# Attention on one core: the numerator's matmuls grouped over two steps, and two small matmul blocks moved a step earlier

## The reference

```python
q = (x @ wq_w + wq_b).reshape(bs, sl, KV_H, FACTOR, HEAD_DIM)
k = (x @ wk_w + wk_b).reshape(bs, sl, KV_H, HEAD_DIM)
v = (x @ wv_w + wv_b).reshape(bs, sl, KV_H, HEAD_DIM)
attn = jnp.einsum('bqhfd,bkhd->bhfqk', q, k) * scale
att = jax.nn.softmax(attn, axis=-1)
a = jnp.einsum('bhfqk,bkhd->bqhfd', att, v)
```

## Time and profile of the kernel before

| | |
|---|---|
| median of three runs | 2871.31 us |
| profiled execution, time | 2874.47 us |
| profiled execution, span from first to last instruction | 2872.7 us |
| busy: PE, DVE, ACT, POOL | 96%, 77%, 53%, 67% of the span |
| attention stage | about 635 to 2345 us |
| granted TensorE clock, 700 to 2300 us | 0.99 to 1.00 of full speed |

### The profile page before, as it was taken

The page is one execution under the profiler, slowest core; times in us unless marked ns, Lnnn a source line. Parts: engine busy times, 40 slices in busy tenths (PEclk is TensorE's granted clock), DMA queues, the critical chain, the costliest instruction groups (busy, mean ns, idle before and its releaser), DMA issues. The chain is left out here.

```text
span 2872.7 us, 48710 instructions
## 1 busy us (share of the span) xinstructions
PE 2771.2 (96%) x14638; PEld 1701.4 (59%) x14638; DVE 2197.9 (77%) x2775; ACT 1520.3 (53%) x2906; POOL 1925.5 (67%) x714
## 2 busy tenths in 40 slices
PE   7999999999999999999999999999999959999997
PEld 4788888874444444444444444444444427888886
DVE  4433333348999999999999999999999967666675
ACT  3211111117766666666666667667666733455443
POOL 2433333218999999999999999999999965111110
PEclk9999999999999999999999999999999979999998
DMA  7544444524433444443344334443434333333331
GB/s 263 180 140 140 139 139 139 155 85 122 95 88 85 94 94 89 86 98 83 88 96 94 89 85 94 92 90 87 98 83 92 65 106 114 111 100 98 110 110 66
DMA packets 167583, 307.60 MB, mean 107 GB/s; under 512 B 50000, under 2 KB 91408, under 8 KB 159376
## 3 DMA queue, kind: packets, MB, share of 16 engines
q1 hardware_dynamic: 158368, 240.05, 28.8%
q0 software_dynamic: 9072, 66.06, 11.3%
HBM read 159.12 MB, written 79.82 MB: 83 GB/s over the span
## 5 line engine op out<-in xcount | busy, mean ns | idle before, releaser
L1006 ACT ACTIVATE p_t<-st_ps 128x512 f32<-128x512 f32 x2048 | 1113.8, 596 | 464.1 <-PE st_ps L1126 392.1
L1026 DVE TENSOR_REDUCE mx<-s_ps 128x1 f32<-128x1024 f32 x1002 | 1172.7, 1209 | 111.8 <-PE s_ps L1100 103.4
L955 POOL TENSOR_TENSOR p_sum<-p_sum,p_t 128x2048 f32<-128x2048 f32 x256 | 1178.8, 4605 | 44.7 <-ACT p_t L1006 28.2
L1126 PE MATMUL st_ps<-q_st,k_st 98*128 98x512 f32 x2048 | 815.8, 438 | 24.5 <-ACT p_t L1006 18.9
L1126 PEld LDWEIGHTS st_ps<-q_st,k_st 98*128 98x128 f32 x2048 | 345.9, 188 | 618.7 <-ACT p_t L1006 515.8
L1100 PE MATMUL s_ps<-k_st,q_st 96*128 96x512 f32 x2004 | 633.3, 397 | 1.8 <-DVE mx L1026 1.5
L1140 PE MATMUL num_ps<-p_t,v_sb 128*32 128x512 f32 x4096 | 547.2, 606 | 0.9 <-ACT p_t L1006 0.9
L1100 PEld LDWEIGHTS s_ps<-k_st,q_st 96*128 96x128 f32 x2004 | 379.2, 189 | 74.2 <-DVE mx L1026 5.1
L495 POOL TENSOR_TENSOR o_lo<-side,o_hi 128x512 fp32r<-128x512 f32 x80 | 104.3, 1304 | 323.6 <-ACT o_hi L465 323.4
L955 POOL TENSOR_TENSOR p_sum<-p_t 128x2048 f32<-128x2048 f32 x64 | 312.6, 4885 | 12.0 <-ACT p_t L1006 12.0
L1041 DVE TENSOR_REDUCE two_sum<-p_t 128x512 f32<-128x1024 f32 x256 | 317.6, 1241 | 3.3 <-DMA p_sum<-two_sum 2.0
(11 more groups left out here) (138 smaller groups left out, 2889.9 us busy)
## 6 DMA issues: line engine op xcount, KB each, us to landing
p_sum<-two_sum POOLq DMA_DIRECT2D x63, 1024.0 KB, 7.0
q_st<-q_hi_d SPq DMA_DIRECT2D x128, 256.0 KB, 4.4
stage<-w_mod SPq DMA_DIRECT2D x48, 512.0 KB, 6.3
q_hi_d<-o_hi SPq DMA_DIRECT2D x64, 256.0 KB, 2.0
q_lo_d<-o_lo SPq DMA_DIRECT2D x64, 256.0 KB, 2.0
q_st<-q_lo_d SPq DMA_DIRECT2D x64, 256.0 KB, 4.1
att_d<-a_sb SPq DMA_DIRECT2D x128, 128.0 KB, 2.3
a_f<-att_d SPq DMA_DIRECT2D x32, 512.0 KB, 4.8
```

What stands on the lines that cost most here:

```text
L955: nc.gpsimd.tensor_tensor(total, before, p_t[:, kt, :, :], ALU.add).then_inc(sum_done, 1)
L1006: nc.scalar.activation(p_t[:, s, c, :], st_ps[:, c % 2, :], ACT.Exp, scale=SCALE)\
L1026: nc.vector.tensor_reduce(mx[:, slot % 2, e:e + 1], s_ps[:, e % 2, :], AX_X, ALU.max)\
L1126: nc.tensor.matmul(st_ps[:, c % 2, :], k_st[:, slot // 2, s * P:(s + 1) * P], q_st[:, slot, jj, h * QW:(h + 1) * QW], start=True, stop=True)\
```

## The change

PE no longer makes one numerator block at the start of each step. At the start of every even step it makes those of the two steps before, one behind the other; odd steps begin with scores 2 and 3 straight away. The turn of the maxima moves from step 5 to step 4 (ACT's part with it, DVE's part to step 5), and the denominator's block from step 7 to step 6. After the last pair both remaining numerator blocks are made. No instruction is added or dropped.

```diff
-    SUM_STEP = 7
+    SUM_STEP = 6
     DIVIDE_STEPS = (1, 2, 3)
     DIVIDE_AFTER = 2
-    TURN_STEP = 5
+    TURN_STEP = 4
@@
                     for s in range(STEPS):
-                        before = (pair, slot, s - 1) if s else (pair - 1, (slot - 1) % QR, STEPS - 1)
-                        if not (below(pair, 1) and s == 0):
-                            add_num(*before)
+                        if s % 2 == 0 and not (below(pair, 1) and s == 0):
+                            before = (pair, slot, s) if s else (pair - 1, (slot - 1) % QR, STEPS)
+                            for back in (2, 1):
+                                add_num(*before[:2], before[2] - back)
                         if s == SUM_STEP and not below(pair, 1):
                             add_sum(pair - 1, (slot - 1) % 2)
                         if s == TURN_STEP and not is_int(pair, NPAIR - 1):
@@
                 pairs(pe, do)
-                add_num(NPAIR - 1, QR - 1, STEPS - 1)
+                for back in (2, 1):
+                    add_num(NPAIR - 1, QR - 1, STEPS - back)
                 add_sum(NPAIR - 1, (NPAIR - 1) % 2)
                 add_two(NPAIR - 1)
```

## The result

The changed kernel takes 2969.36 us (median of four runs, 2965.07 to 2970.97) against 2870.93 us before: a ratio of 1.0337, 95% interval 1.0324 to 1.0350. It is 98 us slower. The forecast was 2974 us.

A forecast was written before the change was run, and what follows sets the result against it. PE's pace and ACT's hand-over through the two banks of `st_ps`, equally late, were taken as the bound. Hand-over's 94 us plus 63 x 0.15 made 103 us, added to 2871: 2974 us, range 2915 to 3030.

The forecast's parts named there:

- Double block to c2: Start of an even step: from first numerator matmul to scores 2, two blocks take 1.85 us, the second costing 0.85.
- The hand-over chain: Odd steps: scores 2 and 3 (c2', c3') wait for ACT's exponentials of c0' and c1', loading at 4.23 and 4.71 us.
- Next block: Two steps between numerator blocks on PE: 6.57 us against 6.20, 0.37 more, 94 us over 255 groups.
- DVE at 0.05 for a whole pair: Fourth entry of an odd step: DVE's backlog reaches it once, by 0.0 to 0.3 us; taken as 0.05 a pair.
- rival 3: Odd steps: DVE becomes the bound, each fourth entry waiting 0.3 us for a maximum; 3042 us, chance 0.08.
- PE's saving: PE's stream: joining two numerator blocks saves 0.37 us in two steps, 6.20 to 5.83.
- The turn: Turn of the maxima moved to step 4: waiting for step 3's last maximum costs 0 to 0.3 us, taken as 0.1.
- The denominator: Denominator's block moved from step 7 to 6: 0.85 us in either place, behind a block both times; no cost.
- Loop edges: Edges of the loop: their cost to PE and ACT stays the same, since no instruction is added.
- Signs: Trace after: blocks 6.5 to 6.6 us apart, odd-step loads idle, PE's share under 0.95, POOL waiting for ACT, pairs 27.6.

The follow-up runs named there:

- after_low: Changed kernel with both matmuls of an entry writing the same half of `s_ps` and the maximum taken of that half alone: 2943.6 us, ratio 1.0246.
- grouped_only: Changed kernel with the turn of the maxima set back to step 5 and the denominator's block to step 7: 2926.5 us, ratio 1.0188.
- odd_order: Changed kernel with one entry matmul of each odd step placed between scores 2 and scores 3: 2952.1 us, ratio 1.0277.
- the twins with four banks: Kernel before and changed kernel, each with four banks for the scores and maxima over half of each row: 2844.9 and 2843.6 us.
- those without POOL's limit: Single-block and grouped kernels with four banks, half maxima, POOL's additions of steps 6 and 7 left out, reciprocal of a constant: 2823.2 and 2721.4 us.
- the first relief of POOL: Single-block and grouped kernels with four banks, half maxima, no POOL additions of steps 6 and 7, multiplication by zero replacing the reciprocal: 2854.9 and 2796.4 us.
- the clean one: Rerun of the first relief of POOL with the reciprocal of a constant replacing the multiplication by zero: 2823.2 us single, 2721.4 us grouped.

## Why the prediction was right

The direction, the size and the mechanism held; that the sum came within 5 us is in part luck, as the terms show. They can be checked one by one against the traces. The table has the time from a step's first numerator matmul to that of two steps later, in us, as the median of all pairs:

| from the block of step | before | changed | changed, `after_low` | `grouped_only` | `odd_order` |
|---|---|---|---|---|---|
| 0 | 6.29 | 6.86 | 6.65 | 6.81 | 6.65 |
| 2 | 6.20 | 6.63 | 6.55 | 6.63 | 6.56 |
| 4 (with the turn) | 6.40 | 6.83 | 6.75 | 6.63 | 6.83 |
| 6 (with the denominator) | 7.11 | 7.49 | 7.41 | 7.11 | 7.48 |
| a pair | 26.00 | 27.81 | 27.36 | 27.18 | 27.52 |

- **Double block to c2**: 1.85 forecast, 1.85 measured (1511.72 to 1513.57).
- **The hand-over chain**: exponential of c0' at 3.58 forecast, 3.57 measured; load of c2' 4.23 and 4.22; load of c3' 4.71 and 4.72. Each figure came from a row of one ordinary step, one denominator step, and nothing else.
- **Next block**: 6.57 forecast, 6.63 measured. Nearly all of the missing 0.06 is in one place. The third entry of the odd step was forecast to wait for nothing; its load waits 0.25 for DVE's maximum at 1517.22, and c0'' starts at 5.85 instead of 5.75. This is the term that the forecast mis-sized. It had DVE at 0.05 for a whole pair; with halved maxima the changed kernel's pair is 0.45 shorter (table), 0.08 in three of its four stretches and 0.21 in that of step 0, where the third entry's load waits longest:

```profile
1510.59 0.19 PEld L1100 LDWEIGHTS s_ps<-k_st,q_st 96*128 96x128 f32 x1 [0.36 <-DVE mx L1026]
```

  The forecast had named entries that wait for DVE as a sign of its rival 3. They do wait, in every odd step, but for 0.24 to 0.36 at the load, of which 0.08 to 0.21 reaches the next block, where the rival had 0.3: 26 us in all, and not its 77. Without DVE's share, two ordinary steps take 6.55, 0.02 below the forecast's 6.57.
- **PE's saving**: 0.37 forecast for two steps. Between the twins with four banks it is 6.12 less 5.79, 0.33, and 0.35 between those without POOL's limit. The Trainium skill, "TensorEngine Tiling (Array Packing)", Key Properties, describes a drain at a change of tiling mode, and these runs agree with a price of that kind.
- **The turn**: 0.1 a pair forecast, none measured: 1.74 to the turn, against a maximum ready at 1.68. This was close. With one block ahead the same move costs 48 us, and the forecast, which reckoned with a double block, did not look at that case.
- **The denominator**: nothing forecast, and behind a block it costs its own length as before. But the forecast compared only one place behind a block with another. The place that the grouping opens up, the head of an odd step, is worth 0.39 to it and 0.20 to the turn, and `SUM_STEP` 7 and `TURN_STEP` 5 would have been there. So the two moves are 43 of the 98 us. The sum was right all the same, because it took every odd step as uncovered, which the moves make true.
- **Loop edges**: "the same after" was wrong, to the good. In the kernel before, c2 started 2.10 behind a single block at a loop's edge (1.00 elsewhere):

```profile
1277.17 1.06 PE L1140 MATMUL num_ps<-p_t,v_sb 128*32 128x512 f32 x8
1279.27 0.99 PE L1126 MATMUL st_ps<-q_st,k_st 98*128 98x512 f32 x2 [1.03 <-ACT p_t L1006]
```

  after the change, 2.13 behind a double block (1.85 elsewhere):

```profile
1309.51 1.92 PE L1140 MATMUL num_ps<-p_t,v_sb 128*32 128x512 f32 x16
1311.64 0.98 PE L1126 MATMUL st_ps<-q_st,k_st 98*128 98x512 f32 x2 [0.21 <-ACT p_t L1006]
```

  In these two the edge holds PE's stream until 2.1 us after the block's start either way, and the second block hides 0.85 of that. Over the 13 edges between the 14 rounds the pairs there are longer than the others by 19 us in sum before and by 6 after: 13 us given back. What PE does in that time no run here shows. The trace puts the wait down to ACT, which had finished before.
- **Signs**: PE's busy share was to fall under 0.95; it is 27.00 of 27.80, 0.97. The others came, or nearly: double blocks 6.63 apart (6.5 to 6.6 forecast), pairs 27.8 (27.6), c2' released 0.05 behind its exponential, and POOL waiting for ACT 2.0 us a pair (122.2 in some 60 pairs).

Together: a pair grew by 1.81 (26.00 to 27.81), 1.36 of it the hand-over's (1.48 forecast) and 0.45 DVE's (0.05 forecast, and 0.1 for the turn). Over 63 pairs it makes 114 us; less 13 for the edges and 6 behind the last numerator matmul, from whose start to the end of the span it was 544.2 us before and is 537.8 after, it comes to 95. The spans of the two traced executions differ by 94 (2872.7 and 2966.9), the medians by 98, since the traced execution of the kernel before was 3 us above its median. The forecast's 103 had DVE too small by more than it had the hand-over too large, 11 us in all, and left out the 19 that the edges and the end gave back; the two went against each other and left it 5 us too high.

## What to carry to other kernels

In a two-bank hand-over between engines, ask what the in-order producer does while the consumer catches up. Work that looks like overhead between the banks' turns may be the cover of the round trip, and moving it away turns hidden latency into a stall, however much it shortens the producer's stream. A stretch of the trace where the suspected bound is absent (here the last pair, without entries, at the same 3.09 us a step) tells whether a second limit stands right behind the first; and work placed where the producer waits is cheap: at the head of an odd step the turn cost nothing (6.63 us for two steps with it and without), the denominator 0.48 (7.11) instead of 0.86 (7.49).

## What the runs showed of the hardware that I had not expected

A DVE multiplication of 128x16 fp32 elements by a constant, from SBUF to SBUF, took 4079 ns in the median of 64 and 161 ns at the least, in the grouped kernel with that edit. The instruction's line in its trace:

```profile
L1055 DVE TENSOR_SCALAR rden_c<-den_t x64: 161/4079/4299, 702.4 to 2278.5; 128x16 f32<-128x16 f32 x64
```

A reciprocal of the same shape in the same place, beside the same additions of POOL, takes 230 ns in the changed kernel:

```profile
L1054 DVE RECIPROCAL rden_c<-den_t x64: 221/230/255, 704.2 to 2441.0; 128x16 f32<-128x16 f32 x64
```

The long ones ended with POOL's addition (1546.76 and 1546.72 in the rows above): 61 of the 64 ran beside one and ended 0.03 to 0.04 us behind it. The Trainium skill, "SBUF — State Buffer", section "SBUF: two separate sides", says that some DVE operations and GpSimd's share a pair of ports that one of them holds for its whole instruction while the other is blocked. The trace agrees with that, with 4.08 us for 0.16 of work. So one small operation put in another's place in an experiment can add a wait of its own: the first relief of POOL read 59 us, the clean one 102.
